# A graph network on one core: preparation in another order, late key scatters, copied parts for the extras, and sums and clears on GpSimd

## What is computed

```python
# three layers; batch norm and relu after the first two
weight = einsum('rb,bio->rio', comp_l, bases_l)
h = einsum('ni,rio->nro', x, weight)
msg = h[src, etype]
norm = 1.0 / maximum(count_of(dst, etype), 1.0)
y = segment_sum(msg * norm, dst) + x @ root_l + bias_l
# then
x = layernorm(x + y)
h = x @ W_in + b_in                     # 128 -> 64
w = deg_inv_sqrt[row] * deg_inv_sqrt[col]
cur = acc = h
for _ in range(3):
    cur = segment_sum(cur[col] * w, row); acc = acc + cur
x = layernorm(x + (acc / 4) @ W_out + b_out)
```

## Time and profile before

| | us |
|---|---|
| median of three runs | 5185.52 (5184.09 to 5193.47) |
| the profiled execution | 5210.32 |
| its span | 5208.6 |
| busy: TensorE (PE) | 3696.4 (71%) |
| busy: VectorE (DVE) | 3216.3 (62%) |
| busy: GpSimd (POOL) | 2705.4 (52%) |
| busy: ScalarE (ACT) | 1086.7 (21%) |

### The profile page before, as it was taken

The page is one execution under the profiler, slowest core; times in us unless marked ns, Lnnn a source line. Parts: engine busy times, 40 slices in busy tenths (PEclk is TensorE's granted clock), DMA queues, the critical chain, the costliest instruction groups (busy, mean ns, idle before and its releaser), DMA issues.

```text
span 5208.6 us, 68902 instructions
## 1 busy us (share of the span) xinstructions
PE 3696.4 (71%) x16076; PEld 2010.5 (39%) x16077; DVE 3216.3 (62%) x8810; ACT 1086.7 (21%) x1906; POOL 2705.4 (52%) x2646
## 2 busy tenths in 40 slices
PE   7116766777678576777776687767767766999996
PEld 3003333333333344444444434444444443454443
DVE  6965455444434666666666646666666667747475
ACT  4000000000003233333333433333333334000000
POOL 0666677667661566666666426666666661000000
PEclk9556666566668788888888898888888888999998
DMA  6011111111115344444444354444444443999995
GB/s 230 14 32 46 45 46 46 46 46 47 45 46 211 93 124 123 123 123 124 124 123 125 116 219 122 122 123 124 121 123 123 124 123 113 368 347 364 338 360 195
DMA packets 416740, 717.16 MB, mean 138 GB/s; under 512 B 98579, under 2 KB 322632, under 8 KB 416111
## 3 DMA queue, kind: packets, MB, share of 16 engines
q1 hardware_dynamic: 332138, 545.45, 29.8%
q0 software_dynamic: 84096, 166.09, 12.5%
q10 hardware_dynamic: 130, 1.20, 0.1%
HBM read 432.25 MB, written 280.06 MB: 137 GB/s over the span
## 4 chain that ended last, share of the span: by engine, by line
PE 53%; issue 18%; POOL 9%; DVE 7%; another core or an unknown queue 7%; DMA 4%; ACT 1%; SPq 1%; DVEq 0%; ACTq 0%; POOLq 0%
PE psum L953 21%; PE psum L1003 11%; PE psum L940 9%; PE psum L929 6%; POOL area L622 6%; PE psum L901 3%; POOL key_list L592 3%; DMA area<-msg_table,visit_src 2%; DMA area<-counts 1%; PE psum L916 1%; PE psum L1016 1%; ACT bufE L672 1%; DVE edge_area L1181 1%; PE psum L1017 1%
## 5 line engine op out<-in xcount | busy, mean ns | idle before, releaser
L622 POOL DMA_INDIRECT area<-msg_table,visit_src x2490 | 2525.0, 1014 | 1427.7 <-issue 608.5
L953 PE MATMUL psum<-area 128*128 128x256 f32 x4980 | 1917.3, 487 | 374.8 <-DMA area<-msg_table,visit_src 143.7
L953 PEld LDWEIGHTS psum<-area 128*128 128x128 f32 x4980 | 1087.0, 238 | 972.2 <-issue 626.9
L1681 DVE TENSOR_TENSOR agg_and<-agg_and,psum 128x256 f32 x1245 | 520.8, 418 | 1160.5 <-PE psum L953 566.6
L672 ACT CAST bufE<-psum 128x512 f16<-128x512 f32 x1507 | 860.4, 587 | 1674.6 <-remote 713.1
L940 PE MATMUL psum<-bufE,carry 128*128 128x512 f16 x1505 | 647.1, 430 | 726.7 <-issue 612.5
L1650 DVE TENSOR_SCALAR area<-iota,agg_and 128x256 f32<-128x256 f32 x2490 | 886.4, 417 | 17.4 <-issue 15.8
L929 PE MATMUL psum<-bufE 128*128 128x512 f16 x1507 | 638.9, 424 | 0.9 <-issue 0.9
L1003 PE MATMUL psum<-area,edge_area 128*64 128x512 f16 (+1 forms) x5733 | 618.9, 371 | 27.0 <-DMA area<-counts 17.2
L940 PEld LDWEIGHTS psum<-bufE,carry 128*128 x1505 | 158.2, 105 | 1138.2 <-issue 1053.5
L1657 DVE TENSOR_SCALAR bufE<-iota,bufD 128x128 f16<-128x128 f16 x1507 | 432.7, 287 | 264.8 <-PE psum L929 147.4
(11 more groups left out here) (334 smaller groups left out, 1648.3 us busy)
## 6 DMA issues: line engine op xcount, KB each, us to landing
area<-counts SPq DMA_DIRECT2D x252, 896.0 KB, 6.8
counts<-bufE SPq DMA_DIRECT2D x1507, 128.0 KB
msg_table<-area SPq DMA_DIRECT2D x147, 512.0 KB, 2.6
area<-msg_table,visit_src POOLq DMA_INDIRECT x2490
agg_and<-counts SPq DMA_DIRECT2D x165, 128.0 KB, 6.7
area<-counts SPq DMA_DIRECT2D x21, 224.0 KB, 3.8
bufE<-inv_sqrt SPq DMA_DIRECT2D x2, 1568.0 KB, 12.5
out<-cur SPq DMA_DIRECT2D x12, 256.0 KB
```

Of the source, the lines that this page charges most:

```text
L622: g.indirect_dma_start(out=msg[:, n % MV, :], out_offset=None, in_=msg_table, in_offset=bass.IndirectOffsetOnAxis(ap=visit_src[:, v:v + 1] ...
L953: t.matmul(psum[:, banks[c % len(banks)], at:at + W2], msg[:, n % MV, :], visit_sel[:, n % SV, :], start=v % 2 == 0, stop=v % 2 == 1).then ...
L1681: v.tensor_tensor(to, to, psum[:, banks[c % len(banks)], at:at + W2], ALU.add).then_inc(visit_added, 1)
```

## The change

- SP issues the edge loads first, the tile ends on a semaphore of their own (`lasts_in`), then bases and comp. The second layer's bases are loaded right after the first table, no longer behind the wait for the last key scatter.
- VectorE no longer makes the first weights at the start but after `plan_visits`; `find_lasts` moves into `pad_windows`, behind the counts.
- TensorE sums the order check before it turns x, and the other sums of the plan before the table.
- GpSimd scatters 98 of the 112 keys (`EARLY`), then gathers the tiles, then scatters the last 14.
- The parts of an extra are copied by ScalarE into one of two buffers; TensorE multiplies them by three matmuls of 64 columns into one of four banks, and VectorE folds two halves instead of three.
- GpSimd makes the residual adds of both norms and clears `sums` and `edge_sums`.

```diff
+EARLY = CHUNKS - 2 * (PAD - 1)
...
-            sp.dma_start(bases_sb[:, :, :], bases[0].rearrange("b i o -> i b o")).then_inc(bases_in, 16)
-            sp.dma_start(comp_sb[:, :], comp...).then_inc(bases_in, 16)
             sp.dma_start(dst_i, dst.rearrange("(p c) -> p c", p=EP)).then_inc(edges_in, 16)
...
             sp.wait_ge(lasts_clear, 1)
             for to, of in last_of_tiles(tile_last_i, dst, 1):
-                sp.dma_start(to, of).then_inc(edges_in, 16)
+                sp.dma_start(to, of).then_inc(lasts_in, 16)
+            sp.dma_start(bases_sb[:, :, :], bases[0].rearrange("b i o -> i b o")).then_inc(bases_in, 16)
+            sp.dma_start(comp_sb[:, :], comp...).then_inc(bases_in, 16)
...
             table(0)
+            sp.wait_ge(weights_ready, 1)
+            sp.dma_start(bases_sb[:, :, :], bases[1].rearrange("b i o -> i b o")).then_inc(bases_in, 16)
             sp.wait_ge(keys_written, 16 * CHUNKS)
             sp.wait_ge(x_turned, NXT)
             sp.dma_start(list_rows, key_list...).then_inc(list_in, 16)
             for layer in range(1, LAYERS):
-                if layer == 1:
-                    sp.wait_ge(weights_ready, layer)
-                    sp.dma_start(bases_sb[:, :, :], bases[layer].rearrange("b i o -> i b o")).then_inc(bases_in, 16)
                 table(layer)
...
             pool.wait_ge(places_ready, 1)
-            place_keys()
+            place_keys(range(EARLY))
             pool.wait_ge(visits_planned, 1)
             pool.wait_ge(rows_out, 16)
             for j in range(VB):
                 g.indirect_dma_start(out=runs[:, j, :, :]...).then_inc(tiles_in, 16)
+            place_keys(range(EARLY, CHUNKS))
...
+            def add_residual(c, other):
+                g.tensor_tensor(agg[:, chunk[c]], xT[:, chunk[c]], other[:, chunk[c]], ALU.add).then_inc(ln_in, 1)
+            pool.wait_ge(visit_added, pairs(LAYERS))
+            for c in range(NB):
+                add_residual(c, agg)
+            pool.wait_ge(deg_out_s, 16)
+            g.memset(bufD[0:H, :], 0.0).then_inc(sums_clear, 1)
+            pool.wait_ge(ln_turned, NB)
+            g.memset(agg[0:H, :], 0.0).then_inc(sums_clear, 1)
+            for c in range(NB):
+                pool.wait_ge(out_biased, c + 1)
+                add_residual(c, cur)
...
+                act.wait_ge(parts_ready, HG * hop + HG)
+                for e in range(NX):
+                    x = NX * hop + e
+                    column = act.value_load(extra_at[0:1, 0, e:e + 1], min_val=0, max_val=(NBLK - 1) * PARTS)
+                    if x >= 2:
+                        act.wait_ge(extras_used, x - 1)
+                    a.copy(extra_parts[:, x % 2, :], parts.rearrange("p b n -> p (b n)")[:, bass.ds(column, PARTS)]).then_inc(extra_parts_ready, 1)
...
-                            if x >= 2:
-                                pe.wait_ge(extras_folded, x - 1)
-                            column = pe.value_load(extra_at[0:1, 0, e:e + 1], min_val=0, max_val=(NBLK - 1) * PARTS)
-                            bank = 4 + 2 * (x % 2)
-                            t.matmul(psum[:, bank, :], flat[:, bass.ds(column, 2 * H)], extra_in[:, x % XR, :], start=True, stop=True)
-                            t.matmul(psum[:, bank + 1, :], flat[:, bass.ds(column + H, 2 * H)], extra_in[:, x % XR, :],
-                                     start=True, stop=True).then_inc(extras_used, 1)
+                            if x >= 4:
+                                pe.wait_ge(extras_folded, x - 3)
+                            pe.wait_ge(extra_parts_ready, x + 1)
+                            for i in range(3):
+                                half = slice(i % 2 * H, i % 2 * H + H)
+                                last = t.matmul(psum[half, 4 + x % 4, :], extra_parts[:, x % 2, i * H:(i + 1) * H], extra_in[:, x % XR, :],
+                                                start=i < 2, stop=i > 0)
+                            last.then_inc(extras_used, 1)
...
-                    fold(to[:, bass.ds(column, BW)], (psum[H:2 * H, bank + 1, :], psum[H:2 * H, bank, :], psum[0:H, bank, :]), extras_folded)
+                    fold(to[:, bass.ds(column, BW)], (psum[H:2 * H, 4 + x % 4, :], psum[0:H, 4 + x % 4, :]), extras_folded)
...
-            link(v.memset(edge_sums, 0.0))
-            link(v.memset(sums, 0.0))
...
+            dve.wait_ge(sums_clear, 2)
             for hop in range(HOPS):
```

More of the change, by code:

```diff
@@ L290, in build @@
         rest = agg_and[:, NP + XR * 256:NP + XR * 256 + HB * H]
-        assert XR * 256 + HB * H <= COLS + 128 - NP
+        AT = NP + XR * 256 + HB * H
+        extra_parts = agg_and[:, AT:AT + PARTS].bitcast(BF16).rearrange("p (s n) -> p s n", n=PARTS)
+        assert AT + PARTS <= COLS + 128
         agg = agg_and[:, 0:NP]
@@ L587, in _, with place_keys @@
             g.memset(norm[:, :], 0.0).then_inc(constants, 1)
-            def place_keys():
-                for k in range(CHUNKS):
+            def place_keys(chunks):
+                for k in chunks:
                     g.indirect_dma_start(out=key_list, out_offset=bass.IndirectOffsetOnAxis(ap=key_address[:, k:k + 1], axis=0),
@@ L758, in _ @@
             pe.wait_ge(constants, CONSTANTS)
+            pe.wait_ge(hist_ready, 1)
+            t.matmul(psum[:, 7, 0:1], ones[0:EP, :], upto_block[:, NBLK:NBLK + 1], start=True, stop=True).then_inc(base_ready, 1)
             pe.wait_ge(rows_in, 32)
@@ L766, in _ @@
                 last.then_inc(x_turned, 1)
-            def sum_descents():
-                pe.wait_ge(hist_ready, 1)
-                t.matmul(psum[:, 7, 0:1], ones[0:EP, :], upto_block[:, NBLK:NBLK + 1], start=True, stop=True).then_inc(base_ready, 1)
             def edges_before():
@@ L982, in hop_sums @@
             def hop_sums(hop):
-                flat = parts.rearrange("p b n -> p (b n)")
                 for w in range(NB):
@@ L1042, in project @@
                 t.matmul(psum[:, 6 + c % 2, :], w_in_sb[:, :], xT[:, chunk[c]], start=True, stop=True).then_inc(proj_mm, 1)
+            sum_ranks()
+            edges_before()
+            spread_blocks()
             pe.wait_ge(x_kept, NXT)
             pe.wait_ge(weights_ready, 1)
-            sum_descents()
-            table_blocks(0, xT, 0, NBLK // 3)
-            sum_ranks()
-            edges_before()
-            table_blocks(0, xT, NBLK // 3, NBLK)
+            table_blocks(0, xT, 0, NBLK)
             root_product(0, xT)
-            spread_blocks()
             spread_ends()
@@ L1125, in _ @@
             link(v.memset(xT[:, N:NP], 0.0))
-            make_weights(0)
-            dve.wait_ge(edges_in, 96)
+            dve.wait_ge(edges_in, 64)
             dve.wait_ge(constants, CONSTANTS)
@@ L1145, in pad_windows @@
                     link(v.tensor_scalar(is_bucket16, bucket16, float(w), 0.0, ALU.is_equal, ALU.add, accum_out=count[0:EP, w:w + 1]))
+                find_lasts()
                 whole = left[0:EP, w13].bitcast(I32)
@@ L1216, in find_lasts @@
                 upto = in_bucket[:, 0:NBLK * PER].rearrange("p (n j) -> p n j", j=PER)
-                link(v.tensor_copy(block, tile_last[:, :, 1]))
-                link(v.tensor_scalar(block, block, 7, None, ALU.logical_shift_right))
+                dve.wait_ge(lasts_in, 32)
+                link(v.tensor_scalar(block, tile_last_i[:, :, 1], 7, None, ALU.logical_shift_right))
                 link(v.tensor_copy(tile_block[:, :], block))
@@ L1290, in rank_link @@
                     dve.wait_ge(rank_step, ranked[0])
+                dve.wait_ge(lasts_in, 32)
+                rank_link(v.tensor_copy(tile_last[:, :, :], tile_last_i[:, :, :]))
                 rank_link(v.tensor_copy(payload[:, :, 1], dst_i))
@@ L1308, in _ @@
                 dve.wait_ge(lasts_reloaded, 32)
-            find_lasts()
+                rank_link(v.tensor_copy(tile_last_i[:, :, 1], tile_last[:, :, 1]))
             link(v.tensor_scalar(bucket_i, src_i, LOW_BITS, None, ALU.logical_shift_right))
@@ L1318, in _ @@
             plan_visits()
+            make_weights(0)
             def group_edges():
@@ L1738, in scale_next, with normalise @@
                     v.tensor_tensor(scaled[:, chunk[c]], of[:, chunk[c]], scale[:, chunk[c]], ALU.mult).then_inc(hop_scaled, 1)
-            def normalise(n, other):
+            def normalise(n):
                 base = NB * n
-                for c in range(NB):
-                    if n:
-                        dve.wait_ge(out_biased, c + 1)
-                    v.tensor_tensor(agg[:, chunk[c]], xT[:, chunk[c]], other[:, chunk[c]], ALU.add).then_inc(ln_in, 1)
                 def find_moments(c):
```

11 lines of the change are left out of this document (5 added, 6 removed).

## The result

| | before | changed |
|---|---|---|
| median | 5187.19 us (5184.09 to 5193.47, 4 runs) | 5096.64 us (5092.36 to 5101.86, 4 runs) |
| the profiled execution (span) | 5210.32 (5208.6) | 5097.2 (5095.5) |
| VectorE busy in it | 3216.3 | 3083.1 |
| ScalarE busy | 1086.7 | 1146.4 |

The ratio is 0.9824, 95% interval 0.9807 to 0.9841: 90.5 us less. The direction was right, the size too small.

What follows compares the result with a forecast made beforehand. It took VectorE, then GpSimd, to bound the preparation, the DMA stream the hops and VectorE the end. Preparation -41.1, first norm -21.5, extras -3, last norm +8 gave -57.6 us: 5128 from a median of 5185.52, range 5100 to 5150.

Steps and rivals of the forecast that it cites:

- Start of the preparation: Preparation up to the key addresses: edges land at 12.3, sort chain starts at 20.0, addresses at 128.9 instead of 159.68 us.
- The long middle and GpSimd: Key addresses to first message gather: edge rows at 294.7, gather at 336.9 instead of 378.03; preparation in all -41.1 us.
- rivals 3 and 4: Table's writes beside GpSimd's scatters: 3, they slow them, 14 us lost, 5142, 11%; 4, scatters stand still, 5206, 2%.
- rival 5: Start of the preparation: something else still holds the sort, its 31 us are lost, 5159 us, 2%.
- First norm: Last visit to first hop: adds and two clears move to GpSimd and stay hidden, -21.5 us.
- Extras: Hops: narrower matmuls save 0 to 24 us, taken as -3 since the DMA stream is full.
- Rival 2: Hops: TensorE, not the DMA engines, sets the pace and the extras bring 24 us, 5107 us, 8%.
- Last norm: End: moments start 4.9 us earlier, but GpSimd's adds hold up VectorE's scaling by 12.7, +8 us.
- Rival 1: End: GpSimd's adds disturb nothing, 12.7 us less, 5115 us, 27%.

Runs made afterwards that it cites:

- e11: e6 with SP's load of x held back until behind VectorE's branch; ratio 0.9764 to the kernel before.
- e4: The changed kernel with the last norm's 13 adds back on VectorE; ratio 0.9823 to the kernel before, end 62.5 us.
- e5: The changed kernel run again without edits, beside the kernel before on one chip; 4688.98 against 4772.80 us, ratio 0.9825.
- e7: The kernel before run again without edits, on the chip of e5; 4772.80 us.
- e6: The changed kernel with the last sums finished inside the last hop and the end's work interleaved by chunk; 4662.19 us, ratio 0.9769 to the kernel before.
- e1: The kernel before with only the change's preparation; 4746.18 against 4781.06 us, ratio 0.992.
- e8: The changed kernel with two of three parts multiplied in the hops' regular blocks, stream of counts unchanged; hops 663.6 us.
- e9: The changed kernel with extras' copied parts multiplied by two 128-column matmuls and folded in three adds; hops 726.8 us.
- e12: The changed kernel with all 112 key scatters ahead of the tile gathers; first message gather at 352.0 us.

## Why the prediction was wrong

**Start of the preparation: mechanism right, 4.3 us short.** The edges landed at 12.8, the check needs neither x nor weights. The term that failed is "then 4.06 us of branch": I moved the branch from a quiet place to one beside x's load and took its length along (e11).

**The long middle and GpSimd: right.** From the addresses to the edge rows 164.7 us (165.8 predicted), tiles kept by 334.8 (331.8), before GpSimd was free. Beside the table's writes the scatters stand 1.75 us apart, as beside the sort before (1.744); rivals 3 and 4 are out. The start did move, so rival 5 is too, though the branch and the load of x that it names did cost 4 us.

**First norm: right**, -20.4 against -21.5. The adds took 1.27 us each, above my 0.5 to 1.2, and stayed hidden below the 2.6 us of a chunk.

**Extras: the step that failed.** It read: "freed from the extras the stream went no faster. So 0 to -24; I take -3 us". It brought 27.5; a hop became 9 us shorter, which the prediction had named as what would prove it wrong (8 us). The comparison was of two stretches that TensorE paced in both. With extras, two groups and two extras are 2.10 MB in 5.63 us, 372 GB/s; without them 1.84 MB in 4.72 us would be 389, but there TensorE also transposes for the next hop, and now and then waits for a load. That 363 and 365 came out alike was an accident; the 363 was read from 40 us only. Two things stood against my reading: TensorE busy 147.91 of 150 us, which I set aside, and TensorE's waits in that stretch, none of them for a load, which the prediction doesn't weigh. Rival 2, to which I gave 8%, was right in its mechanism, and its 24 us came near the 27.5.

**Last norm: right**, +7.7 against +8, and for the reason given: 11 operations held up by about 1 us each, where I had 11 adds of 1.15. The terms came out as -3.8 and +11.3, against -4.9 and +12.7; that their sum fits to 0.3 us is partly luck. Rival 1 is refuted by e4. The rule that a VectorE instruction with two SBUF inputs and a GpSimd instruction that reads SBUF exclude each other (the Trainium skill, SBUF — State Buffer, Who interferes with whom) agrees with this trace: 0.68 us became 1.64 to 1.75.

**The sum.** -57.6 predicted; 24.5 more in the extras, 4.3 and 1.1 less in the preparation and the norm, 0.3 less lost at the end: -77.0. From the median of 5185.5 that is 5108.5. Another 12 us separate it from the measured 5096.6. On one chip with both kernels profiled the visits differed by 1.6 us (e5, e7) and the medians by 83.8; the ratio of the first measurement has an interval of 18 us. I take the 12 us as part of that, but the runs don't settle it: no kernel isolates what an execution of the visits varies by.

## What to carry to other kernels

When a matmul engine and a stream both read as nearly full, look whether the consumer ever waits for a load: if not, the stream isn't the bound. Here neither its busy share near 1 nor its queue's waits for buffers told the two cases apart. To know what a stream can do, leave out a part of the arithmetic and see what rate it reaches. Work that is moved to another engine should be placed beside neighbours that it doesn't hold up (here VectorE operations that read PSUM, as in e6, not those with two SBUF inputs), and a time taken along with moved code (a branch, a load) holds only where its new surroundings are as quiet as the old.

## What the runs showed of the hardware that I had not expected

- The busy share of the DMA engines read 0.99 at 365 GB/s, 1.01 at 391 and 1.03 at 408.
- A branch of VectorE took 3.8 to 4.1 us away from the load of x and 7.9 to 8.3 beside it.
- A register load on TensorE for each of 165 extras cost nothing (707.0 against 706.5 and 707.7).
- GpSimd's add of 128x512 in f32 takes 1.26 to 1.27 us undisturbed, VectorE's 0.61.
- The visits took 3516 to 3535 us on two chips (e1 to e8), at a granted clock of 0.97 to 0.99 in the second and third layer, and 3965 to 3976 on a third (e9 to e12), at 0.85 to 0.87. The two first profiles, 3963 and 3927, had 0.84 to 0.86. No other stage followed the chip.
